# A decoder layer on one core: two PSUM banks exchanged, the split of turned x moved from GpSimd to ScalarE and VectorE, the last turns written out

## The reference

```python
x = x + _L0_attn_ref(_layernorm(x), Wq, bq, Wk, bk, Wv, bv, Wo, bo)
x = x + _L0_xattn_ref(_layernorm(x), ctx, wq, bq, wkv, bkv, wp, bp)   # q = _qdq(x) @ _qdq(wq).T + bq ; out = _qdq(o) @ _qdq(wp).T + bp
x = x + _L0_ffn_ref(_layernorm(x), router_w, w_gate, w_up, w_down)
```

## Time and profile before

| what | value |
|---|---|
| time, median of 3 runs | 1690.42 us (1682.73 to 1698.85) |
| the profiled execution | 1691.19 us, span of its instructions 1689.4 us |
| busy TensorE, VectorE, ScalarE, GpSimd | 1414.6, 1179.7, 944.6, 734.6 us |
| mean granted TensorE clock | 0.935 |

### The profile page before, as it was taken

One profiled execution on the slowest core, in us unless ns is written; L12 is line 12 of the kernel. 1 busy time (PEld: TensorE's weight loads), 2 busy tenths in 40 slices (PEclk: granted clock), 3 DMA queues, 4 the chain that ended last, 5 costly groups with the idle time before them and its releaser, 6 DMA issues.

```text
span 1689.4 us, 36382 instructions
## 1 busy us (share of the span) xinstructions
PE 1414.6 (84%) x11243; PEld 1061.0 (63%) x11276; DVE 1179.7 (70%) x3050; ACT 944.6 (56%) x3313; POOL 734.6 (43%) x718
## 2 busy tenths in 40 slices
PE   5499898998878999898999998889854988888895
PEld 3377676776666677766777676667642655555564
DVE  4878787888777888888888878877752444444453
ACT  2367666766656776666776656656741333333332
POOL 2123444444443454445354445334442444555565
PEclk9599999999999999999999999999976999999997
DMA  6755322222211110111110110110087999999964
GB/s 198 298 203 214 124 100 93 92 91 102 94 44 36 33 37 31 31 56 31 31 37 31 37 50 31 31 31 26 14 272 246 273 274 273 275 278 284 281 102 52
DMA packets 164529, 204.33 MB, mean 121 GB/s; under 512 B 40245, under 2 KB 122421, under 8 KB 164480
## 3 DMA queue, kind: packets, MB, share of 16 engines
q1 hardware_dynamic: 125568, 165.86, 29.8%
q0 software_dynamic: 38912, 37.87, 11.0%
HBM read 136.19 MB, written 130.29 MB: 158 GB/s over the span
## 4 chain that ended last, share of the span: by engine, by line
DVE 26%; PE 21%; DMA 19%; issue 17%; another core or an unknown queue 7%; ACT 5%; POOL 1%; DVEq 1%; POOLq 0%; SPq 0%; ACTq 0%
DMA out<-x,slots 19%; PE bank L525 10%; ACT probs L990 3%; DVE small L1257 3%; PE bank L531 3%; PE bank L553 3%; DVE small L1290 2%; DVE chosen L1354 2%; DVE wide_a L1326 2%; PE bank L507 2%; DVE roped L1323 1%; DVE x L1333 1%; DVE wide_b L1498 1%; PE bank L560 1%
## 5 line engine op out<-in xcount | busy, mean ns | idle before, releaser
L990 ACT ACTIVATE probs<-bank,small 128x128 f32<-128x128 f32 x1024 | 362.8, 384 | 127.7 <-DVE small L1290 101.3
L1783 POOL DMA_INDIRECT routed<-row,slots x248 | 257.5, 1038 | 130.8 <-issue 74.2
L1738 POOL TENSOR_TENSOR small<-small,half 128x1 f32<-128x1 f32 x96 | 54.2, 565 | 544.6 <-DVE small L1262 543.5
L1858 POOL DMA_INDIRECT out<-x,slots x128 | 198.4, 1550 | 197.5 <-DMA out<-x,slots 146.1
L990 ACT ACTIVATION_READ_ACCUMULATOR probs<-bank,small 128x1 f32 x1024 | 229.7, 224 | 0.0
L984 ACT ACTIVATE probsT<-bank 128x512 f32<-128x512 f32 x256 | 144.1, 612 | 108.2 <-PE bank L553 89.8
L1290 DVE TENSOR_REDUCE small<-bank 128x4 f32<-128x512 f32 x256 | 166.6, 683 | 46.4 <-remote 38.7
L553 PE MATMUL bank<-idf,probs 128*128 128x128 f32 x1024 | 155.6, 287 | 4.7 <-ACT probs L990 3.1
L553 PEld LDWEIGHTS bank<-idf,probs 128*128 128x128 f32 x1024 | 126.9, 150 | 35.6 <-issue 8.8
L1693 DVE TENSOR_SCALAR slots<-pairs 128x1 uint32<-128x1 f32 x128 | 13.7, 149 | 188.8 <-DMA out<-x,slots 181.8
L525 PE MATMUL bank<-w_k_hi,xT_hi 128*128 128x512 f32 x128 | 63.9, 499 | 49.2 <-ACT xq8T L984 30.6
(11 more groups left out here) (248 smaller groups left out, 3943.6 us busy)
## 6 DMA issues: line engine op xcount, KB each, us to landing
w_gate_up<-in_w_gate SPq DMA_DIRECT2D x128, 192.0 KB
w_gate_up<-in_w_up SPq DMA_DIRECT2D x128, 192.0 KB
w_down<-in_w_down SPq DMA_DIRECT2D x128, 192.0 KB
routed<-empty_row SPq DMA_DIRECT2D x16, 1280.0 KB, 11.7
x_in<-in_x SPq DMA_DIRECT2D x32, 256.0 KB
xn<-in_xT_in SPq DMA_DIRECT2D x32, 256.0 KB
ctx_sb<-in_ctxT_in SPq DMA_DIRECT2D x32, 256.0 KB
x_res<-in_x SPq DMA_DIRECT2D x32, 256.0 KB
```

Of the source, the lines that this page charges most:

```text
L990: last = act.activation(probs[:, g, j * P:(j + 1) * P], bank[:, b, j * P:(j + 1) * P], ACT.Exp, bias=negated[:, h:h + 1], **({"accum_out": ...
L1738: pool.tensor_tensor(c["r0"], c["v"], half[:, :], ALU.pow).then_inc(g_pow[kind], 1)
L1783: pool.indirect_dma_start(routed, bass.IndirectOffsetOnAxis(ap=slots_of(m)[:, k:k + 1], axis=0), row_of(m)[:, :], None, bounds_check=SLOTS ...
L1858: pool.indirect_dma_start(out.rearrange("b p (h c) -> (b p h) c", h=2), bass.IndirectOffsetOnAxis(ap=place_of[k % 2][:, half_:half_ + 1], ...
```

## The change

- `turn_cross_attention` and `cross_average` use bank 5 instead of 4, `turn_quantised_x` and `copy_quantised_x` bank 1 instead of 5. `queries_a` no longer waits for `cross_average`; `keys_a` waits for it instead of for `copy_quantised_x`.
- `turned_x_hi` and `turned_x_lo` go from GpSimd. `x_hi` on ScalarE stands between `copy_cross_keysT` and `exp_1`, `x_lo` on VectorE between `cross_average` and `max_2`. SP's load of the next turned x waits for `x_lo`.
- `self_scores` waits for the second step of find_slots, `cross_scores` for the first of second_sum.
- On SP, five experts' weights are issued in turn B + 2 after q, k and v are done, and three in turn B + 3; before, two in turn B + 2 after these and two more were done, and six in turn B + 4.
- The last turns are written out: TensorE's last three, the others' last two. VectorE takes three copies and one norm that ScalarE did; GpSimd puts the norm's power of tile 32 behind the first two descriptors of tile 31's scatter.

```diff
             def load_turned_x(m):
-                reached(sp, g_xT, m - 1, 2, 2)
+                reached(sp, d_xT, m - 1, 1, 1)
...
                 if cur == B + 2:
-                    for projected in (p_q, p_k, p_v, p_xk, p_o):
+                    for projected in (p_q, p_k, p_v):
                         sp.wait_ge(projected, 3 * B)
-                    for k in range(2):
+                    for k in range(5):
+                        load_weights(k, k)
+                if cur == B + 3:
+                    for projected in (p_xk, p_o):
+                        sp.wait_ge(projected, 3 * B)
+                    for k in range(5, 8):
                         load_weights(k, k)
                 if cur == B + 4:
-                    for k in range(2, 8):
-                        load_weights(k, k)
...
             def self_scores(m):
-                reached(pe, d_r2, m - 3, 6, 6)
+                reached(pe, d_r2, m - 3, 6, 2)
...
-                turn(4, xatt, p_xo)
+                turn(5, xatt, p_xo)
...
-                turn_bf16(5, xq8, p_q8T)
+                turn_bf16(1, xq8, p_q8T)
...
             def queries_a(m):
-                reached(pe, g_xT, m, 2, 1)
+                reached(pe, a_xT, m, 1, 1)
+                project(4, xT_hi, xT_lo, "q", 0, True, False).then_inc(p_q, 1)
+
+            def keys_a(m):
                 reached(pe, d_xatt, m - 3, 2, 2)
-                project(4, xT_hi, xT_lo, "q", 0, True, False).then_inc(p_q, 1)
-
-            def keys_a(m):
-                reached(pe, a_q8T, m - 2, 1, 1)
                 project(5, xT_hi, xT_lo, "k", 0, True, False).then_inc(p_k, 1)
...
             def cross_scores(m):
-                reached(pe, d_x2, m - 1, 2, 2)
+                reached(pe, d_x2, m - 1, 2, 1)
...
+            def x_hi(m):
+                reached(act, s_xT, m, 16, 16)
+                reached(act, p_v, m - 1, 3, 3)
+                copy(flat(xT_hi), xn[:, :], a_xT)
...
+            def x_lo(m):
+                reached(dve, a_xT, m, 1, 1)
+                dve.tensor_tensor(flat(xT_lo), xn[:, :], flat(xT_hi).bitcast(F32), ALU.subtract).then_inc(d_xT, 1)
...
+            cross_output(B - 1)
+            cross_scores(B)
+            turn_cross_probs_1(B)
+            turn_cross_probs_0(B)
+            turn_normed(B - 1)
+            turn_cross_probs_2(B)
+            turn_cross_probs_3(B)
+
+            pe.wait_ge(a_xpT, 4 * B)
+            weigh_turned(5, 1, xv_sb, p_xpv)
+            weigh_cross_3(B)
+            weigh_cross_0(B)
+            weigh_cross_2(B)
+            turn_cross_attention(B)
+            logits(B - 1)
+            turn_quantised_o(B)
+            positions(B - 1)
+            cross_output(B)
+            turn_normed(B)
+            logits(B)
+            positions(B)
...
-            def turned_x_hi(m):
-                reached(pool, s_xT, m, 16, 16)
-                reached(pool, p_v, m - 1, 3, 3)
-                apart(pool)
-                pool.tensor_copy(flat(xT_hi), xn[:, :]).then_inc(g_xT, 1)
-
-            def turned_x_lo(m):
-                reached(pool, g_xT, m, 2, 1)
-                pool.tensor_tensor(flat(xT_lo), xn[:, :], flat(xT_hi).bitcast(F32), ALU.subtract).then_inc(g_xT, 1)
...
+            bias_first_sum(B)
+            number_tokens(B - 1)
+            number_tokens(B)
+            scatter(B - 1, 0, 2)
+            ffn_power(B)
+            scatter(B - 1, 2, TOPK)
+            scatter(B)
```

More of the change, by code:

```diff
@@ L913, in _ @@
                 body(cur)
-            for cur in range(B + 1, B + 6):
+            for cur in range(B + 1, B + 3):
                 body(cur)
+            positions(B - 2)
+            weigh_cross_1(B - 1)
+            weigh_cross_3(B - 1)
+            weigh_cross_0(B - 1)
+            weigh_cross_2(B - 1)
+            turn_cross_keys(B)
+            turn_cross_attention(B - 1)
+            cross_values_b(B)
+            turn_quantised_x(B)
+            cross_values_c(B)
+            cross_queries(B)
+            cross_values_a(B)
+            turn_quantised_o(B - 1)
+            turn_cross_queries(B)
+            cross_output(B - 1)
[18 more added lines that the diff above has]
+            positions(B)
             def turn_rows(n, k, use):
@@ L1069, in copy_quantised_x @@
                 reached(act, p_q8T, m, 1, 1)
-                copy(flat(xq8T), bank_bf16(5), a_q8T)
+                copy(flat(xq8T), bank_bf16(1), a_q8T)
             def exp_2(m):
@@ L1155, in body @@
                     copy_cross_keysT(cur - 3)
+                if has(cur - 1):
+                    x_hi(cur - 1)
                 if has(cur - 2):
@@ L1208, in _ @@
                 body(cur)
-            for cur in range(B + 1, B + 6):
+            for cur in range(B + 1, B + 4):
                 body(cur)
+            cross_exp_1(B)
+            cross_exp_2(B)
+            cross_exp_3(B)
+            act.wait_ge(p_xpT, nth(B, 4, 3))
+            copy(probsT[:, 2, :], bank[:, 4, :], a_xpT)
+            copy_cross_probs_3(B)
+            copy_turned_attention(B)
+            router_exp(B - 1)
+            copy_quantised_o(B)
+            ffn_normed(B)
+            copy_normed(B)
+            router_exp(B)
             def copy_rows(n, k):
@@ L1590, in body @@
                     cross_average(cur - 4)
+                if has(cur - 1):
+                    x_lo(cur - 1)
                 if has(cur - 2):
@@ L1675, in _ @@
                 body(cur)
-            for cur in range(B + 1, B + 6):
+            for cur in range(B + 1, B + 4):
                 body(cur)
+            round_o(B - 1)
+            quantise_o(B - 1)
+            copy_cross_values(B)
+            second_sum(B - 1)
+            cross_max_0(B)
+            cross_max_1(B)
+            cross_max_2(B)
+            cross_max_3(B)
+            ffn_statistics(B - 1)
+            ffn_rsqrt(B - 1)
+            dve.wait_ge(d_ln["ffn"], 7 * (B - 1))
+            dve.tensor_scalar(row_of(B - 1)[:, 0:D], x2[:, :], ln["ffn"]["r"], ffn_shift, ALU.mult, ALU.add).then_inc(a_normed, 1)
+            for n, (g, b) in enumerate(((1, 0), (0, 2))):
+                dve.wait_ge(p_xpT, nth(B, 4, n + 1))
+                dve.tensor_copy(probsT[:, g, :], bank[:, b, :]).then_inc(a_xpT, 1)
+            dve.wait_ge(p_x3T, B - 1)
+            dve.tensor_copy(x3T[:, :], bank[:, 3, :]).then_inc(a_x3T, 1)
+            cross_average(B)
+            scale_o(B)
+            router_max(B - 1)
+            round_o(B)
+            quantise_o(B)
+            route(B - 1)
+            shares(B - 1)
+            find_slots(B - 1)
+            second_sum(B)
+            ffn_statistics(B)
+            ffn_rsqrt(B)
+            router_max(B)
+            route(B)
+            shares(B)
+            find_slots(B)
             def multiply(n, k):
@@ L1777, in self_power, with scatter @@
                 rsqrt("self")
-            def scatter(m):
+            def scatter(m, first=0, end=TOPK):
                 reached(pool, d_r2, m, 6, 6)
                 apart(pool)
-                for k in range(TOPK):
+                for k in range(first, end):
                     pool.indirect_dma_start(routed, bass.IndirectOffsetOnAxis(ap=slots_of(m)[:, k:k + 1], axis=0), row_of(m)[:, :], None,
@@ L1793, in bias_residual, with body @@
                 pool.tensor_tensor(x_res[:, :], x_res[:, :], att_bias[:, :], ALU.add).then_inc(g_res, 1)
-            def body(cur, split=True):
+            def body(cur):
                 if has(cur - 3):
@@ L1805, in body @@
                     cross_power(cur - 3)
[L1806 to L1809, removed]
                 if has(cur - 1):
@@ L1834, in _ @@
                 pool.tensor_copy(dst, src).then_inc(s_init, 1)
-            body(2, split=False)
+            body(2)
             pool.iota(row[:, D:ROW:2], pattern=[[0, E]], base=-P, channel_multiplier=1,
```

14 lines of the change are left out of this document (6 added, 8 removed).

## The result

The changed kernel takes 1798.77 us (median of four runs, 1793.03 to 1809.6) where the kernel before took 1686.58 in the same comparison: a ratio of 1.068, 95% interval 1.062 to 1.073. The forecast was 1657, the range 1620 to 1700. The measured time lies outside it, on the slower side, which had been given a chance of 0.14.

The account below looks back on a forecast made before the run. Bound: a loop of waits from find_slots through the scatter and VectorE's work, 35.76 us a pass, 28 passes. Loop -29.4, last turns -5.5, setup +0.7 make -34.2 us: 1657.0 us forecast, range 1620 to 1700.

Parts of the forecast that it names:

- the release: In each pass, the moment about 1.5 us after the last scatter descriptor when TensorE's held signals come out.
- The gain inside it: In the loop of waits, VectorE's cast and m01 get 1.33 us shorter; an undisturbed pass goes from 35.76 to 34.4 us.
- the sum: Total of the 28 passes, 1009 us against 1038.6 (-29.4), with last turns -5.5 and setup +0.7: -34.2 us.
- a fallen clock: In 16 passes TensorE's clock falls; each priced at +1.5 us over an undisturbed one, 35.9 us.
- late news: Slower rival: earlier scatter queues TensorE's signals behind more descriptors, 4.5 us per added late pass, twelve giving 1711 us; chance 0.13.
- the relaxed wait: self_scores after find_slots' second step saves TensorE about 0.6 us behind positions, outside the loop; taken as 0.
- The split's added work: x_hi on ScalarE (0.62 us) and x_lo on VectorE (0.68 us) fall into existing waits: 0, bounds 0 to 19 us.
- The port: Rival: x_lo on VectorE holds a scatter descriptor 0.68 us in every pass, +19, 1676 us; chance 0.13.
- Banks: TensorE's waits at queries_a (1.23 us) and keys_a (1.33 us) go, but become one at turn_probs_1: gain 0.
- The undivided wait: One TensorE wait of about 2.7 us at turn_probs_1, expected to bring the clock down in more passes.
- Last turns: After the loop, earlier weight loads and written-out turns bring tile 32's scatter 5.5 us earlier; bounds 0 and 12 us.
- Setup: Before the loop, the second tile's load and what queues behind it on SP wait for x_lo: +0.7 us (0 to 1.5).

Follow-up runs that it names:

- after_hold_scores: The changed kernel, but GpSimd starts the scatter only when TensorE has signalled the last of the pass's four self scores; 1700.5 us, ratio 1.008.
- after_pool_split: The changed kernel with the split of turned x back on GpSimd at its old place, all else as changed; 1681.5 us, ratio 0.997.
- after_halves: The changed kernel with the scatter in two halves, four descriptors after the scores are signalled, four after cross_output; 1675.3 us, ratio 1.005.
- before_relax: The kernel before with self_scores waiting for the second step of find_slots instead of the sixth, nothing else; 1667.4 us, ratio 1.006.

## Why the prediction was wrong

*The bound.* Right: the loop from find_slots through the scatter and the release, and that TensorE's signals are late under the descriptors. The gain inside it was right too: cast and m01 at 0.18 us. The one pass in which the scatter did not come first took 34.3 us against 34.4, but that agreement is luck. There copy_cross_values starts at 167.77, 1.87 us before the last descriptor ends, and not 1.5 us after it; it is ScalarE's copy of xo8, at 171.10, that waits for the release, and VectorE then waits 2.27 us for the cross output. From find_slots to find_slots, as the 34.4 were worked out, this pass takes 33.3 us.

*The step that failed* is in the sum: "8 passes at 34.4, 16 with a fallen clock at 35.9, and 4 as late as the 41 us ones". The changed kernel has one of the first kind, one of 36.0, and 26 of the last. The mechanism was named, as the rival late news, with its reason (find_slots 1.3 us earlier against TensorE), with a price of 4.5 us a pass and worked out for up to twelve more such passes, 1711 us. Its reason applied to every pass, so its price belonged in the sum, not among the chances. 22 more late passes at 4.5 us are 99 us; and the 26 took (1143.7 - 34.3 - 36.0) / 26 = 41.3 us each and not 39.9, 36 us more. Together 135: the whole distance from the 1009 us of the sum to 1143.7. The state is also a harder one than the one named. In a pass of 41.1 us of the kernel before VectorE hears the scores after 1.08 us of waiting, and the quantised x is held past the last descriptor (ScalarE waits 6.49 us); now the scores themselves are late, and all behind them.

What would have shown it beforehand: the scores' end stood 0.55 us behind the first descriptor's start, and the change moved one by 1.3 us and the other by 0.6. The prediction costed the relaxed wait as time "outside the loop", and the earlier scatter at nothing. It followed the instructions that VectorE and TensorE wait for in order, and not what the scatter, once earlier, lies over. (A small slip beside this: the 34.2 us are taken from the profiled execution; from the median, 1690.4, they give 1656.2 and not 1657.0.)

*The split's added work* was taken as nothing, and nothing speaks against it, though no run takes it out by itself: in the late pass x_hi stands just ahead of 6.43 us in which ScalarE idles, and x_lo's 0.68 us ahead of VectorE's wait of 1.74 us for the cross output. The port's price of 0.68 us was not tested there, since x_lo starts 0.83 us after the last descriptor; in after_hold_scores, where it lies beside one, it did not come (1.02 us, where the descriptor at the same place took 1.22 in after_pool_split with no x_lo). The Trainium skill's "SBUF — State Buffer", section Who interferes with whom, names casts among the instructions that can contend with GpSimd; the cast of 1.26 us beside GpSimd's split and 0.18 without agrees. Of its rule on two inputs, that x_lo could hold a descriptor was the prediction's inference: the same section reports that tensor_tensor, which x_lo is, was seen not to stall a DMA, and no run here shows that it does.

*Banks.* Gain 0, as taken: the ratio is 1.058 without them and 1.068 with, if anything a loss. The undivided wait came, but at keys_a, of 3.81 us, for the cross_average that the prediction had over by then; at turn_probs_1 TensorE waits 1.18 us. The clock is below 1.00 in 27 passes of 28, and 0.92 or less in 26, against 18 and five before; what of the 41 us is the clock's was not measured by itself.

*Last turns.* -5.5 us forecast. In the changed kernel's profile tile 32's scatter starts 1382.45 - 1299.1 = 83.35 us after the start of these turns, before 1279.61 - 1195.9 = 83.71: 0.4 us. The wait of 3.29 us for the store went; in its place second_sum(31) waits 3.00 us for a signal of TensorE, the last 1.76 of them after its matmuls had ended (1342.96), while the scatter of tile 30 runs. So a late signal took back the gain of this wait, where the prediction had let the next engine's work follow at once; where the rest of the 5.5 us went is not shown.

*Setup.* +0.7 forecast, -1.9 measured (155.4 against 157.3). The four terms: loop +105.1, last turns -0.4, setup -1.9, the rest -1.0, together 101.8.

What stays open is why TensorE's signals come late at all, and which of them. The count of descriptors alone does not say it (after_halves), nor the order of the scores: they come at once in before_relax, and the turned probabilities then do not; and in the kernel before a pass of 41.1 us has its scores 0.57 us ahead of the first descriptor, as the quick pass has. Whether the writing of the descriptors holds the signals or the transfers that they start, no run tells apart.

## What to carry to other kernels

When an edit makes an engine quicker, list what that engine releases and what the released work will now lie over; here a microsecond saved on VectorE started a 10 us scatter on GpSimd ahead of TensorE's scores instead of in their middle. A rival whose condition the change itself brings about in every pass is no rival but the forecast. Before keeping a long burst of indirect transfers at the earliest place it can go, try it one wait later: a wait added gave back 5.5% of the time here.

## What was not expected of the hardware

TensorE's signals come late by amounts that the matmuls don't explain, while GpSimd writes the descriptors of an indirect DMA. VectorE's wait for the scores is none in after_hold_scores, 1 to 2 us where they end half a microsecond behind the first descriptor's start, and 5.3 us on average where they start behind it and the descriptors go on (138.2 us over 26 passes). Beside that, the kernel before varies between the five chips by 1.9% (1656.4 to 1688.3 us, each taken at one time), as much as many an edit is worth.
